# Four MoE layers and two scans on one core: routing in halves, mixer weights requested in the MoE ahead, a moved output projection, another first sequence, and residual rows summed by TensorE

## The reference

```python
x = x + 0.5 * moe_gated(LN(x))      # m0
x = x + mamba_simple(LN(x))         # s0, the gated scan
x = x + 0.5 * moe_gated(LN(x))      # m1
x = x + 0.5 * moe_capacity(LN(x))   # m2
x = x + mamba_heads(LN(x))          # s1, the selective scan
x = x + 0.5 * moe_capacity(LN(x))   # m3
```

## Time and profile before

| what | value |
|---|---|
| median of 3 runs | 3280.31 us |
| the profiled execution: its own time | 3282.22 us |
| the profiled execution: its span | 3279.4 us |
| PE busy | 2580.4 us (79%) |
| DVE busy | 2222.7 us (68%) |
| POOL busy | 2018.0 us (62%) |
| ACT busy | 1575.7 us (48%) |
| mean granted TensorE clock | 0.91 |

### The profile page before, as it was taken

How to read it: one execution, slowest core, us unless ns; L and a number is a source line. 1 busy time by engine, 2 the same in 40 slices (tenths; PEclk the granted TensorE clock), 3 DMA queues, 4 the chain that set the end, 5 groups by cost and what they waited for, 6 DMA issues and landing times. The chain is left out here.

```text
span 3279.4 us, 43901 instructions
## 1 busy us (share of the span) xinstructions
PE 2580.4 (79%) x12400; PEld 1850.5 (56%) x12400; DVE 2222.7 (68%) x3998; ACT 1575.7 (48%) x2668; POOL 2018.0 (62%) x1643
## 2 busy tenths in 40 slices
PE   5799994996689999348996678788877875579782
PEld 4599993443579999327995233333332322559672
DVE  5656663786766666683332699999999998653333
ACT  4433333884533333333333667567577662443330
POOL 0377771232057776305772789999999784335776
PEclk9999997998599999569998899999999999589997
DMA  6111112100411111422332689889888886312333
GB/s 180 32 48 48 46 48 56 39 26 1 135 37 48 46 47 40 134 72 61 87 87 43 243 291 310 278 296 305 285 291 301 288 300 207 103 40 76 92 90 85
DMA packets 287326, 429.78 MB, mean 131 GB/s; under 512 B 59196, under 2 KB 196799, under 8 KB 287200
## 3 DMA queue, kind: packets, MB, share of 16 engines
q1 hardware_dynamic: 251744, 357.54, 33.1%
q0 software_dynamic: 35456, 70.86, 9.3%
HBM read 367.71 MB, written 62.39 MB: 131 GB/s over the span
## 5 line engine op out<-in xcount | busy, mean ns | idle before, releaser
L683 POOL DMA_INDIRECT m_rows<-rows_in,m_source x568 | 554.0, 975 | 588.6 <-SPq L580 222.2
L1593 PE MATMUL s_y_ps<-s_prod,ident 128*128 128x512 f32 x1024 | 522.0, 634 | 214.3 <-DVE s_prod L1880 214.3
L1558 POOL TENSOR_TENSOR s_dBu<-s_du,s_B_row 128x1024 f32<-128x1024 f32 x256 | 602.4, 2359 | 84.6 <-DVE s_dA L1873 71.1
L1873 DVE TENSOR_TENSOR_SCAN s_dA<-s_dA,s_dBu 128x1024 f32<-128x1024 f32 x256 | 585.6, 2287 | 44.3 <-POOL s_dBu L1558 44.3
L721 PE MATMUL m_A_ps<-m_rowsT,m_own 128*128 128x256 f32 x2272 | 569.0, 383 | 2.1 <-ACT m_rowsT L763 1.1
L737 PE MATMUL m_Y_ps<-m_own,m_hid 128*128 128x128 f32 x4544 | 556.1, 276 | 3.6 <-issue 3.6
L737 PEld LDWEIGHTS m_Y_ps<-m_own,m_hid 128*128 128x128 f32 x4544 | 531.4, 192 | 5.7 <-issue 5.6
L1593 PEld LDWEIGHTS s_y_ps<-s_prod,ident 128*128 128x128 f32 x1024 | 180.9, 195 | 523.3 <-DVE s_prod L1880 325.9
L773 ACT ACTIVATE m_act_a<-m_A_ps,m_own 128x256 f32<-128x256 f32 x568 | 238.5, 471 | 434.7 <-PE m_A_ps L721 318.9
L721 PEld LDWEIGHTS m_A_ps<-m_rowsT,m_own 128*128 128x128 f32 x2272 | 414.9, 193 | 48.8 <-ACT m_rowsT L763 1.9
L1694 ACT ACTIVATE s_dA<-s_delta,s_decay 128x1024 f32<-128x1024 f32 x256 | 286.0, 1118 | 311.0 <-DVE s_prod L1880 306.2
(11 more groups left out here) (241 smaller groups left out, 3543.9 us busy)
## 6 DMA issues: line engine op xcount, KB each, us to landing
s_B_row<-s_bc_rows SPq DMA_DIRECT2D x256, 512.0 KB, 5.7
s_C_row<-s_bc_rows SPq DMA_DIRECT2D x256, 512.0 KB, 6.0
rows_out<-m_y_sb SPq DMA_DIRECT2D x142, 128.0 KB
rows_in<-m_xs SPq DMA_DIRECT2D x64, 256.0 KB, 2.3
m_rows<-rows_in,m_source POOLq DMA_INDIRECT x568
s_got<-rows_by_token SPq DMA_DIRECT2D x16, 512.0 KB, 5.0
m_got<-rows_by_token SPq DMA_DIRECT2D x32, 256.0 KB, 3.9
rows_by_token<-m_y_sb,m_target POOLq DMA_INDIRECT x284
```

The costliest lines, as they stand in the source:

```text
L683: pool.indirect_dma_start(rows[:, b % AHEAD, r, :], None, c.rows_in, bass.IndirectOffsetOnAxis(source[:, 2 * b + r:2 * b + r + 1], 0)).the ...
L1558: nc.gpsimd.tensor_tensor(dBu[q % RING][:, :], du[s % 2][:, h, :], B_row[q % RING][:, :], ALU.mult).then_inc(dBu_ready, 1)
L1593: ins = nc.tensor.matmul(y_ps[:, at(cc, 512)], c.ident[:, :], prod[q % 2][:, at(cc, 512)], start=(n == 0), stop=(n == NS - 1))
L1873: nc.vector.tensor_tensor_scan(dA[q % 2][:, :], dA[q % 2][:, :], dBu[q % RING][:, :], 0.0, ALU.mult, ALU.add).then_inc(scanned, 1)
```

## The change

1. Routing: the logits go to two PSUM tensors of 32 tiles each; softmax and best two are done half by half. In the not gated kind the first half's subtraction stands before the last two groups' statistics on DVE, and its exponential before the last two groups' rows on ACT.
2. The block map is worked out with one block on a partition (an integer AND with 7 in place of the rounds), spread over the partitions by a product with the identity and one matmul of ones into `tot_ps`, and copied to `block_pack`.
3. The scans' weights and their semaphore are allocated around the MoE ahead of the scan (`gated_weights`, `selective_weights`: the loads and memsets are those of before, unchanged). POOL zeroes at the start of that MoE, SP requests behind the expert weights (m0: 16 transfers, m2: 16).
4. Gated scan: PE runs in, z, low, then out, wide, turn, wide; `y` has two buffers; DVE's add_out stands behind scan.
5. Selective scan, window s = -1: conv, xd and dt of the first half, then of the second, with other slots. The first half's B and C rows are stored at slot 16 and loaded at once, the second half's at slot 26. Sequence 0's first `soften` runs on DVE.
6. Selective scan, out rows: PE puts x into the bank by an identity matmul (float32, 512 columns) and sums the projection onto it; ACT copies the bank to x in slots 2 and 3 (`take_out`); DVE's add_out is gone.

The diff, cut to its core:

```diff
-            link(nc.gpsimd.iota(blk_i[:, :], pattern=[[BLK, NBLK + 2]], base=0, channel_multiplier=0))
+            link(nc.gpsimd.iota(blk_i[:, :], pattern=[[0, 1]], base=0, channel_multiplier=BLK))
...
+                def softmax(part, step):
+                    ts = at(part, NT // 2)
+                    if step == 0:
+                        dve.wait_ge(logits_done, (part + 1) * NG // 2)
+                        link(nc.vector.tensor_copy(L[:, ts, :], lps3[part]))
+                        link(nc.vector.tensor_reduce(m[0][:, ts], L[:, ts, :], AX.X, ALU.max))
+                        nc.vector.tensor_tensor(t8[:, ts, :], L[:, ts, :], over_experts(m[0][:, ts]), ALU.subtract).then_inc(logits_shifted, 1)
+                    else:
+                        dve.wait_ge(exp_done, part + 1)
+                        link(nc.vector.tensor_reduce(ind[:, ts], u8[:, ts, :], AX.X, ALU.add))
+                        link(nc.vector.reciprocal(rank[:, ts], ind[:, ts]))
+                        link(nc.vector.tensor_tensor(L[:, ts, :], u8[:, ts, :], over_experts(rank[:, ts]), ALU.mult))
...
+                    if g == NG - 2 and not gated:
+                        softmax(0, 0)
...
+                for part in range(2):
+                    if gated:
+                        dve.wait_ge(logits_done, (part + 1) * NG // 2)
+                        link(nc.vector.tensor_tensor(L[:, at(part, NT // 2), :], lps3[part],
+                                                     gate_b[:, :].unsqueeze(1).to_broadcast([P, NT // 2, E]), ALU.add))
+                    else:
+                        if part == 1:
+                            softmax(1, 0)
+                        softmax(part, 1)
+                    best_two(part)
...
-                link(nc.vector.tensor_tensor(passed[:, :, :], c.block_row[:, :].unsqueeze(2).to_broadcast([P, NBLK + 2, S * E]),
-                                             run_end[:, :, :].rearrange("p i e -> p (i e)").unsqueeze(1).to_broadcast([P, NBLK + 2, S * E]),
-                                             ALU.is_ge))
-                link(nc.vector.tensor_reduce(bmap[:, :], passed[:, :, :], AX.X, ALU.add))
...
-                for i in range(1, S):
-                    link(nc.vector.tensor_scalar(round_done[:, :], bmap[:, :], float(E), float(-E), ALU.is_ge, ALU.mult))
-                    link(nc.vector.tensor_tensor(bmap[:, :], bmap[:, :], round_done[:, :], ALU.add))
-                link(nc.vector.tensor_scalar(block_pack[:, :], bmap[:, :], float(E - 1), None, ALU.min))
+                link(nc.vector.tensor_scalar(passed[:, :], run_end[:, :, :].rearrange("p i e -> p (i e)"), c.block_row[:, 0:1], None, ALU.is_le))
+                link(nc.vector.tensor_reduce(bmap[:, :], passed[:, :], AX.X, ALU.add))
+                link(nc.vector.tensor_copy(bmap_i[:, :], bmap[:, :]))
+                link(nc.vector.tensor_scalar(bmap_i[:, :], bmap_i[:, :], E - 1, None, ALU.bitwise_and))
+                link(nc.vector.tensor_copy(bmap[:, :], bmap_i[:, :]))
+                nc.vector.tensor_scalar(spread_map[:, :], c.ident[:, :], bmap[:, 0:1], None, ALU.mult).then_inc(map_ready, 1)
...
+                dve.wait_ge(map_spread, 1)
+                link(nc.vector.tensor_copy(block_pack[:, :], tot_ps[:, 0:NBLK + 2]))
...
+                pe.wait_ge(map_ready, 1)
+                nc.tensor.matmul(tot_ps[:, 0:P], c.ones_bf[:, :], spread_map[:, :], start=True, stop=True).then_inc(map_spread, 1)
...
+                def exponentials(part):
+                    act.wait_ge(logits_shifted, part + 1)
+                    nc.scalar.activation(u8[:, at(part, NT // 2), :], t8[:, at(part, NT // 2), :], ACT.Exp).then_inc(exp_done, 1)
...
+                if ahead is not None:
+                    ahead.clear()
...
                 loads(sp)
+                if ahead is not None:
+                    ahead.request(sp)
...
-            for s, uses in ((v + 1, (("in", range(N_DVE)),)), (v - 1, (("out", range(2)),)),
-                            (v + 1, (("in", range(N_DVE, HALVES * HC)), ("z", range(HALVES * HC)), ("low", range(HC)),
-                                     ("wide", range(HALVES * HC)))),
+            for s, uses in ((v + 1, (("in", range(HALVES * HC)), ("z", range(HALVES * HC)), ("low", range(HC)))),
+                            (v - 1, (("out", range(2)),)), (v + 1, (("wide", range(HALVES * HC)),)),
                             (v + 2, (("turned", range(2)),)), (v + 1, (("wide", range(HALVES * HC, 2 * HALVES * HC)),)),
                             (v + 3, (("sum", range(4)),))):
                 if has(s):
...
-                    project_in(v + 1, range(N_DVE))
+                    project_in(v + 1, range(HALVES * HC))
+                    project_z(v + 1)
+                    project_low(v + 1)
                 if has(v - 1):
                     project_out(v - 1)
                 if has(v + 1):
-                    project_in(v + 1, range(N_DVE, HALVES * HC))
-                    project_z(v + 1)
-                    project_low(v + 1)
                     project_wide(v + 1, 0)
                 if has(v + 2):
                     turn_rows(v + 2)
...
-                if s > 0:
+                if s > 1:
                     for g in range(2):
-                        Use("out", s - 1, g).read(dve)
...
-                    add_out(v - 1)
                 if has(v + 2):
                     statistics(v + 2)
                 if has(v):
                     scan(v)
+                if has(v - 1):
+                    add_out(v - 1)
...
-                order += [("dt", t, 0), ("dt", t, 1), ("xd", t, 2), ("xd", t, 3), ("dt", t, 2), ("dt", t, 3)]
+                if t == 0:
+                    for h in range(HALVES):
+                        order += [(role, 0, h * HC + cc) for role in ("conv", "xd", "dt") for cc in range(HC)]
+                else:
+                    order += [("conv", t, k) for k in range(3)] + [("xd", t, 0), ("xd", t, 1), ("conv", t, 3)]
+                    order += [("dt", t, 0), ("dt", t, 1), ("xd", t, 2), ("xd", t, 3), ("dt", t, 2), ("dt", t, 3)]
...
+            def store_bc(t, halves):
+                for h in halves:
+                    for cc in range(HC):
+                        Use("xd", t, h * HC + cc).taken(sp)
+                    sp.dma_start(bc_rows[t % 2, h, :, :, :, :].rearrange("k j n t -> (k j n) t"),
+                                 xd[PAIR:3 * PAIR, h, :]).then_inc(bc_stored, 16)
...
+                if t == 0:
+                    if i == 16:
+                        store_bc(0, (0,))
+                        sp.wait_ge(bc_stored, 16)
                         for q in range(RING):
                             load_B(q)
                             load_C(q)
-                if s == -1 and i == ALLN - 1:
-                    for q in range(RING, RING + 2):
-                        load_B(q)
-            sp.wait_ge(loaded, LOADS)
+                    if i == 26:
+                        store_bc(0, (1,))
+                        sp.wait_ge(bc_stored, 32)
+                        for q in range(RING, RING + 2):
+                            load_B(q)
+                elif t is not None:
...
-                if t is not None and 26 <= i < 30:
+                if t is not None and t > 0 and 26 <= i < 30:
...
+                    use.fill(pe)
+                    nc.tensor.matmul(use.ps[:, :], c.ident[:, :], c.x[:, at(s * 2 + g, GRP), :].rearrange("p j d -> p (j d)"),
+                                     start=True, stop=False)
                     pe.wait_ge(y_gated, s * HALVES + HALVES)
-                    use.fill(pe)
                 for j in range(2 * part, 2 * part + 2):
                     for h in range(HALVES):
                         ins = nc.tensor.matmul(use.ps[:, at(j, P)], y[:, h, at(g * GRP + j, P)], w_out[:, h, :],
-                                               start=(h == 0), stop=(h == HALVES - 1))
+                                               start=False, stop=(part == 1 and j == 3 and h == HALVES - 1))
                 if part == 1:
                     ins.then_inc(use.full, 1)
 
...
-            XD_AT, DT_AT = (16, 17, 22, 23), (20, 21, 24, 25)
-            CONV_AT = (9, 10, 11, 12, 14, 15, 18, 19)
-
             def slot(s, t, i):
+                XD_AT, DT_AT = (16, 17, 22, 23), (20, 21, 24, 25)
+                CONV_AT = (9, 10, 11, 12, 14, 15, 18, 19)
+                if s == -1:
+                    XD_AT, DT_AT = (13, 14, 21, 22), (15, 16, 23, 24)
+                    CONV_AT = (9, 10, 11, 12, 17, 18, 19, 20)
...
+            def take_out(s, g):
+                use = Use("out", s, g)
+                use.read(act)
+                nc.scalar.copy(c.x[:, at(s * 2 + g, GRP), :], use.ps[:, :].rearrange("p (j d) -> p j d", j=GRP)).then_inc(use.free, 1)
...
-            CONV_AT, SILU_AT, XD_AT, DT_AT = (11, 13, 16, 20), (13, 20), (17, 18, 23, 24), (21, 22, 26, 27)
             SUM_AT = (27, 29, 30, 31)
 
             def slot(s, t, i):
```

(17 more changed lines are left out.)

351 lines of the change are left out of this document (186 added, 165 removed).

## The result

The changed kernel takes 3234.68 us (median of 4 runs, 3232.1 to 3238.2) against 3280.42: a ratio of 0.9862, interval 0.9845 to 0.9879. Forecast were 3230 and a range of 3219 to 3243; the time lies in it, 4.7 over the point. Its four runs spread over 6.1 us, those of before over 2.1; where that comes from is one of the findings. The profiled execution took 3235.93 us with a span of 3233.9, so 45.5 less span than before.

A forecast was written before the change was run, and what follows sets the result against it. No engine bounds the whole; DVE is busy 931.8 of 945.0 us in the selective scan's steps. Terms a to g sum to 50.1 us, taken from 3280.3: 3230.2, rounded to 3230, range 3219 to 3243.

The forecast's parts named there:

- a: Gated routing in halves, m0 and m1: last logits to `chosen` 3.3 us shorter in each, 6.6 in all.
- c: Block map with one block on a partition: 5.5 us less in m2 and in m3, 11.0 in all.
- d: Scan weights requested ahead, during the MoE before: 9.4 us less in the gated scan, 11.4 in the selective scan.
- b: Not gated routing in halves: 2.4 us less in m2 and 3.7 in m3, 6.1 in all.
- e: Moved out projection in the gated scan: window length unchanged, 0 us, bounds −4 to +4.
- f: Reordered first sequence of the selective scan: 2.1 us less beyond the weights' gain, bounds −2 to +5.
- g: Selective scan's out-row additions moved from DVE to TensorE: 3.5 us less, bounds −0.7 to +7.7.
- rival 1: Gated scan: PE's 1.85 us idle gap gets filled and 6 windows shorten, 12 less, 3218; chance 0.12.
- rival 2: Collisions: PE and ACT give back all of g, first sequence gains nothing beyond d; 3236.5, up to 3240; chance 0.20.
- rival 3: Table loads with a drain: ACT stands 1.38 us longer at each of three places, 3234.3; chance 0.03.
- rival 4: Scan weights land late or hold up the expert weights, so d gives nothing; 3251; chance 0.03.
- rival 5: PE stays at 1.2 GHz in slots 1 to 5 of each selective window: 17 us a window, 3349; chance 0.04.

The follow-up runs named there:

- the run with C first: Changed kernel with both identity matmuls in slot 0 and SP issuing each step's C row ahead of the B row; 3487.24 us, ratio 0.9906.
- the changed kernel's second run: The changed kernel run again without edits, on a slower chip, beside the variants; 3483.43 us against 3523.15 for the kernel before, ratio 0.9886.
- run 180: Not a run's label: 180 counts the scans beside a POOL instruction in the changed kernel's second run, which took 3483.43 us, ratio 0.9886.

## Why the prediction was right, and where it was off

**Right in size:** a, c, d and m3's part of b, to 0.7 us each, since their prices were rows of the same instructions and their place a chain that nothing covered. e came out in its mechanism, with PE's gap moved and an undisturbed window the same (28.9 and 28.87); that its stage differs by 0.0 is luck, as first to last scan is 1.9 longer, by one window at 0.94, and the pieces ahead of it and behind it are 1.8 shorter. f and g came out within 0.6, but not by their own working.

**b, m2, 2.4 forecast, 0.5 found.** The two terms of the sum hold: the three instructions make their round of the loop 1.22 longer (7.25 against 6.03 and 6.04; forecast 1.35), and ACT's exponential and table load make the piece behind it 0.96 to 0.99 longer (9.78 against 8.82 and 8.79; forecast 1.1). What failed is that the sum has nothing else in it: DVE's waits for gathered rows in this loop add up to 6.4 and 6.7 us in the two profiles with the whole routing and to 7.4 to 8.5 in the twelve with halves. Part of them stands ahead of the inserted instructions; why they grow is open.

**g, forecast 3.5, found 4.1 before against after and 1.8 by taking it back.** The term mis-sized was the identity matmul: 0.86 each at the half level, taken as a quarter of `reduce`. But `reduce` has two matmuls, which the trace shows as four instructions, so one is two instructions: 1.92 busy at the half level for the first of a window, 1.02 at the full one for the second. By the forecast's own working with this size (2.6 in place of 1.72, the same lead of 1.3) the wait would be 1.5 a window; it is 0.5 to 1.0 in the mean of seven (3.5 to 6.9 in all, forecast 4.2). Two errors cancel here, and what the second is was not measured. And the saving is bounded otherwise than I wrote: even without that wait nothing is won, as the C rows and then POOL come next.

**f, forecast 2.1, found 1.5.** The working took a half-level clock in one step. What the runs show in its place is a stretch of 49.8 to 58.4 with the same instructions, which goes with the clock's level. Beside the 55.1 of before, this is a gain of 5.3 to a loss of 3.3: that 1.5 came out near 2.1 is luck. Four of the eleven profiles are past the 56 us that the prediction names as a sign of being wrong.

**Not in the sum:** 2.7 at the start of the expert blocks (47.5 to 50.3 in four layers). The twelve variants' profiles, with each of the edits and without it, have 45.0 to 49.0, so it belongs to the scatter of an execution. The total was thus 4.6 of span over the forecast, chiefly this and m2.

**The rivals.** The gated scan's gap did not close (rival 1). Of the collisions (rival 2) PE's wait came, but did not eat all of g. No drain showed behind a table load (rival 3). The transfers were covered (rival 4): taking them back costs 19.2 in place. Of rival 5 the mechanism is there, but elsewhere: not at the selective windows' start, where the clock rose as before, but in the gated scan (1.7 a window) and the first sequence (up to 8.6).

## What to carry to other kernels

An instruction chain that other engines wait for can be priced to 0.2 us from rows of the same instructions (a, c and m3's part of b); an edit in a loop where several engines are near their bound can't, since the time goes to the next one (here PE, then the C rows' transfer, then POOL). Where PE has gaps, compare variants stage by stage and with the granted clock beside: a single total hides edits of 5 us behind the clock, which moved the gated scan and the first sequence by 8.6 each. Know how much a stage scatters in executions with the same code before you read an edit from it. Before work is moved off the bounding engine, look at how late its feeds are already.

## What was not expected of the hardware

- Half-level stretches of the granted clock come back in every middle window of the gated scan in some executions (four windows of 30.61 and one of 29.61, all at 0.94, with the whole routing) and in none in another (four of 28.9 and one of 27.9, all at 1.00, with the old block map), with the same code in that scan.
- Two of the three chips ran m0's expert blocks 16% slower (443 against 381 us; 450 in the last set of runs) and the other stages alike; the cause was not looked for.
- A DVE instruction of 8 columns, 0.17 otherwise, took 0.8 to 2.2 in the six windows of the run with C first, each time until 0.03 behind the end of POOL's dBu. The Trainium skill ("SBUF — State Buffer", "SBUF: two separate sides") has an exclusive lock on a port pair that DVE and GpSimd share, held for a whole instruction; on DVE's side it is taken in a 2-port mode, or by an instruction with two inputs in SBUF against a GpSimd one that reads SBUF. The wait of this instruction, which has one input, would agree if it runs in such a mode, which no trace here shows. DVE's scan and product have two inputs in SBUF, and there the trace does not agree: in the changed kernel's second run 180 scans wholly beside a POOL instruction and 73 beside none have the same mean, 2.29, and so have 170 and 80 products, 1.22.
